# A third buffer of xs, moved bias sums, and v and the output product as three fp32r passes

## The reference

```python
x = x + 0.5 * ffn(layernorm(x))           # ffn: sum of 8 selected 256x256 adapters, gated, plus bias
x = x + attn(layernorm(x))                # an RWKV block, below
x = x + 0.5 * ffn(layernorm(x))

# attn(x):
h = layernorm(x, ln1_g, ln1_b); hh = time_shift(h)
xk, xv, xr = (h * m + hh * (1 - m) for m in (tm_k, tm_v, tm_r))
k, v, sr = xk @ Wk.T, xv @ Wv.T, sigmoid(xr @ Wr.T)
x = x + (sr * wkv(time_decay, time_first, k, v)) @ Wo.T     # wkv: a recurrence over the 512 tokens
h = layernorm(x, ln2_g, ln2_b); hh = time_shift(h)
xk, xr = (h * m + hh * (1 - m) for m in (cm_k, cm_r))
kv = square(relu(xk @ Wck.T)) @ Wcv.T                       # 256 -> 1024 -> 256
return x + sigmoid(xr @ Wcr.T) * kv
```

## Time and profile before

| | us |
|---|---|
| median of 3 runs (442.34, 442.79, 445.81) | 442.79 |
| profiled execution, whole time | 446.01 |
| its span, first to last instruction | 444.1 |
| PE busy | 428.9 (97%) |
| DVE busy | 379.5 (85%) |
| ACT busy | 298.8 (67%) |
| POOL busy | 179.6 (40%) |

### The profile page before, as it was taken

One profiled execution on the slowest core, in us unless ns is written; L12 is line 12 of the kernel. 1 busy time (PEld: TensorE's weight loads), 2 busy tenths in 40 slices (PEclk: granted clock), 3 DMA queues, 4 the chain that ended last, 5 costly groups with the idle time before them and its releaser, 6 DMA issues. The chain is left out here.

```text
span 444.1 us, 6141 instructions
## 1 busy us (share of the span) xinstructions
PE 428.9 (97%) x2014; PEld 335.3 (76%) x2014; DVE 379.5 (85%) x764; ACT 298.8 (67%) x558; POOL 179.6 (40%) x164
## 2 busy tenths in 40 slices
PE   8989999989999999999999899999999999999996
PEld 8865875578858885798759785788569875988985
DVE  3989988979989998999899998999899989976235
ACT  1158979874779568884889477965886487926510
POOL 1535063426271645445363627154543436133011
PEclk9999999969999999999999999999999999999998
DMA  6991010001000200011001100010001000000101
GB/s 199 384 397 41 1 47 0 0 2 50 0 0 1 95 1 1 0 49 48 1 0 47 50 1 1 0 47 2 0 2 47 1 1 0 26 22 1 47 2 48
DMA packets 15970, 18.51 MB, mean 42 GB/s; under 512 B 1082, under 2 KB 13634, under 8 KB 15938
## 3 DMA queue, kind: packets, MB, share of 16 engines
q1 hardware_dynamic: 14538, 17.05, 10.8%
q10 hardware_dynamic: 1400, 1.07, 0.9%
HBM read 13.92 MB, written 4.19 MB: 41 GB/s over the span
## 5 line engine op out<-in xcount | busy, mean ns | idle before, releaser
L448 PE MATMUL pair<-wcv_sb,kk 128*128 128x256 f32 x448 | 100.5, 380 | 0.0
L448 PEld LDWEIGHTS pair<-wcv_sb,kk 128*128 128x128 f32 x448 | 84.5, 191 | 10.9
L1224 POOL TENSOR_TENSOR x2b<-xs,bias_bc 128x512 f32<-128x512 f32 (+1 forms) x16 | 20.2, 1265 | 97.8 <-DVE xs L1047 48.6
L418 PE MATMUL pair<-xck_hi,wck_hi 128*128 128x512 f32 x128 | 57.9, 452 | 0.0
L422 PE MATMUL pair<-xck_lo,wck_hi 128*128 128x512 f32 x128 | 50.6, 395 | 0.0
L419 PE MATMUL pair<-xck_hi,wck_lo 128*128 128x512 f32 x128 | 50.6, 395 | 0.0
L617 ACT ACTIVATE h<-pair,vec 128x512 f32<-128x512 f32 x16 | 11.6, 774 | 45.7 <-PE pair L319 45.7
L673 ACT ACTIVATE kk<-pair 128x512 f32<-128x512 f32 x64 | 36.4, 593 | 8.6 <-PE pair L422 8.6
L677 ACT ACTIVATE kk<-kk 128x512 f32<-128x512 f32 x64 | 37.8, 639 | 0.5
L1264 POOL TENSOR_TENSOR xs<-x,xa 128x512 f32<-128x512 f32 x16 | 20.3, 1270 | 42.1 <-DVE xa L978 38.6
L1250 POOL TENSOR_TENSOR xr<-xr,h 128x512 f32<-128x512 f32 x16 | 18.6, 1181 | 41.5 <-ACT xr L718 41.5
(11 more groups left out here) (149 smaller groups left out, 1050.7 us busy)
## 6 DMA issues: line engine op xcount, KB each, us to landing
x<-in_x_dram SPq DMA_DIRECT2D x8, 512.0 KB, 3.5
out_dram<-xs SPq DMA_DIRECT2D x15, 256.0 KB, 2.1
xt<-in_xt_dram SPq DMA_DIRECT2D x4, 512.0 KB, 7.8
work<-in_ffn_w_dram ACTq DMA_DIRECT2D x4, 256.0 KB, 4.9
work<-in_ffn_w_dram SPq DMA_DIRECT2D x4, 256.0 KB, 5.0
kk<-in_wck_dram SPq DMA_DIRECT2D x1, 1024.0 KB, 10.1
xs<-in_xt_dram SPq DMA_DIRECT2D x2, 512.0 KB, 11.2
wcv_sb<-in_wcv_dram SPq DMA_DIRECT2D x1, 1024.0 KB, 13.0
```

Source lines behind the costliest of these rows:

```text
L418: nc.tensor.matmul(key_bank(n), wck_hi[:, h, cols], xck_hi[:, h, :], start=h == 0, stop=False)
L448: last = nc.tensor.matmul(bank_of("kv", e, i)[:, t % TB * C:(t % TB + 1) * C], kk[:, n, tok:tok + P], wcv_sb[:, n, :], start=n == 0, stop= ...
L1224: nc.gpsimd.tensor_tensor(dst, tile, bias_bc[:, :].rearrange("p (a c) -> p a c", a=1).broadcast_to([P, tiles, C]), ALU.add).then_inc(done, 1)
```

## The change

- `xs` has three buffers (`XS = 3`); the waits on the stores follow.
- v of sequences 1 to 7 becomes three fp32r passes. ACT makes `xv_hi` (`value_input_high`), DVE `xv_lo` (`value_input_rest`), both in two halves. The weights are split once (`setup_wv`, `value_weight_rest`).
- The output product of sequences 1 to 7 becomes three fp32r passes: `rwkv_hi` on ACT (`output_input_high`), `rwkv_lo` on DVE (`output_input_rest`). On PE it moves from behind four parts of value tile 0 to behind six.
- On DVE `gate_input_rest` (xcr_lo) moves from behind the exponent scans to ahead of x2t_lo; `add_second` is split around rwkv_lo.
- On ACT the squares of the keys move back, the relu of keys 6 and 7 ahead of the time gate, and the two gate tanh apart.
- On POOL the bias sum of x2 half 0 is released by xcr_lo, that of x half 0 by the last sum scan (`aa_done`), that of x half 1 by rwkv_lo.
- Several new tiles lie in the place of others (`in_place_of`), which adds waits.

```diff
+    XS = 3
@@ PE, front_v, for f > 0 @@
+                for o in range(CH):
+                    take(pair_of("v", f), o, t1_done, 2 * f + o + 1)
+                    cols = slice(o * P, (o + 1) * P)
+                    for h in range(CH):
+                        if o == 0:
+                            pe.wait_ge(xv_hi_done, 2 * (f - 1) + h + 1)
+                        nc.tensor.matmul(bank_of("v", f, o), wv_hi[:, h, cols], xv_hi[:, h, :], start=h == 0, stop=False)
+                        nc.tensor.matmul(bank_of("v", f, o), wv_lo[:, h, cols], xv_hi[:, h, :], start=False, stop=False)
+                        if o == 0:
+                            pe.wait_ge(xv_lo_done, 2 * (f - 1) + h + 1)
+                        last = nc.tensor.matmul(bank_of("v", f, o), wv_hi[:, h, cols], xv_lo[:, h, :], start=False, stop=h == CH - 1)
@@ PE, output_product, for f > 0 @@
+                pe.wait_ge(rwkv_lo_done, 2 * (f - 1) + 2)
+                for i in range(BANKS):
+                    take(pair_of("o", f), i, xa2_done, 2 * f + i + 1)
+                    for t in range(TB):
+                        last = three_passes(bank_of("o", f, i)[:, t * C:(t + 1) * C], i * TB + t, rwkv_hi, rwkv_lo, wo_hi, wo_lo)
@@ PE, the loop over e @@
-                channel_values(e, 0, range(HB // 2))
+                channel_values(e, 0, range(HB - 2))
                 if has(f):
                     output_product(f)
-                channel_values(e, 0, range(HB // 2, HB))
+                channel_values(e, 0, range(HB - 2, HB))
@@ ACT @@
+            def value_input_high(f):
+                for h in range(CH):
+                    act.wait_ge(xv_done, 2 * f + h + 1)
+                    if h == 0:
+                        act.wait_ge(gated_done, 2 * (f - 1) + 2)
+                    nc.scalar.activation(xv_hi[:, h, :], xv[:, h, :], ACT.Copy).then_inc(xv_hi_done, 1)
+            def output_input_high(f):
+                act.wait_ge(r_ps, 2 * f + 2)
+                for h in range(CH):
+                    act.wait_ge(rwkv_done, 2 * f + h + 1)
+                    nc.scalar.activation(rwkv_hi[:, h, :], rwkv[:, h, :], ACT.Copy).then_inc(rwkv_hi_done, 1)
@@ DVE @@
+            def value_input_rest(f):
+                for h in range(CH):
+                    dve.wait_ge(xv_hi_done, 2 * (f - 1) + h + 1)
+                    nc.vector.tensor_tensor(xv_lo[:, h, :], xv[:, h, :], xv_hi[:, h, :].bitcast(F32), ALU.subtract).then_inc(xv_lo_done, 1)
+            def output_input_rest(f):
+                for h in range(CH):
+                    dve.wait_ge(rwkv_hi_done, 2 * (f - 1) + h + 1)
+                    nc.vector.tensor_tensor(rwkv_lo[:, h, :], rwkv[:, h, :], rwkv_hi[:, h, :].bitcast(F32), ALU.subtract).then_inc(rwkv_lo_done, 1)
@@ POOL, the loop over e @@
                 if has(e - 1):
+                    pool.wait_ge(xcr_lo_done, 2 * e + 2)
+                    bias_to_x2(e - 1, 0)
+                if has(f):
                     mix_r(f)
                     hold_exponents(f)
-                if has(e - 1):
-                    if has(f):
-                        pool.wait_ge(aa_done, 2 * f + 2)
-                    bias_to_x2(e - 1, 0)
                 if has(f + 1):
-                    pool.wait_ge(rwkv_done, 2 * f + 2)
+                    pool.wait_ge(aa_done, 2 * f + 2)
                     bias_to_x(f + 1, 0)
+                    pool.wait_ge(rwkv_lo_done, 2 * (f - 1) + 2)
                     bias_to_x(f + 1, 1)
```

More of the change, by code:

```diff
@@ L76, in build @@
         x1 = [sb(f"x1_{i}", [P, NT, C]) for i in range(X1)]
-        xs = [sb(f"xs_{i}", [P, NT, C]) for i in range(2)]
+        xs = [sb(f"xs_{i}", [P, NT, C]) for i in range(XS)]
         xa = sb("xa", [P, NT, C])
@@ L121, in build @@
         xcr = sb("xcr", [P, CH, T])
+        xcr_lo = in_place_of("xcr", "xcr_lo", [P, CH, T])
         kk = sb("kk", [P, HB, T])
@@ L128, in build @@
         rwkv = sb("rwkv", [P, CH, T])
+        rwkv_hi, rwkv_lo = in_place_of("xr", "rwkv_hi", [P, CH, T]), in_place_of("rwkv", "rwkv_lo", [P, CH, T])
+        xv_hi, xv_lo = in_place_of("thr", "xv_hi", [P, CH, T]), in_place_of("xv", "xv_lo", [P, CH, T])
         work = sb("work", [P, 8 * CH * PAD])
@@ L152, in build @@
         xt_loaded = [sem(f"xt_loaded_{b}") for b in range(B)]
-        stored = [sem(f"stored_{i}") for i in range(2)]
+        stored = [sem(f"stored_{i}") for i in range(XS)]
         bn_done = {k: sem(f"bn_done_{k}") for k in kinds}
@@ L294, in _ @@
                 sp.wait_ge(x3_done, 2 * LAST + j + 1)
-                sp.dma_start(some_tiles(tok_dram(out, LAST), j), some_tiles(xs[LAST % 2], j)).then_inc(stored[LAST % 2], 16)
-            sp.wait_ge(stored[(LAST - 1) % 2], 16 * BANKS * (B // 2))
-            sp.wait_ge(stored[LAST % 2], 16 * (BANKS * (B // 2 - 1) + len(LAST_PARTS)))
+                sp.dma_start(some_tiles(tok_dram(out, LAST), j), some_tiles(xs[LAST % XS], j)).then_inc(stored[LAST % XS], 16)
+            for i in range(XS):
+                sp.wait_ge(stored[i], 16 * sum(len(LAST_PARTS) if b == LAST else BANKS for b in range(i, B, XS)))
         @block.tensor
@@ L330, in to_tokens, with three_passes @@
                     last.then_inc(filled, 1)
-            def three_passes(dst, t):
+            def three_passes(dst, t, own_hi, own_lo, w_hi, w_lo):
                 tok = slice(t * P, (t + 1) * P)
-                passes = [(x2t_hi[:, h, tok], w[:, h, :]) for h in range(CH) for w in (ffn_hi, ffn_lo)]
-                passes += [(x2t_lo[:, h, tok], ffn_hi[:, h, :]) for h in range(CH)]
+                passes = [(own_hi[:, h, tok], w[:, h, :]) for h in range(CH) for w in (w_hi, w_lo)]
+                passes += [(own_lo[:, h, tok], w_hi[:, h, :]) for h in range(CH)]
                 for j, (own, other) in enumerate(passes):
@@ L344, in second_tokens @@
                     for t in range(TB):
[L345 removed]
+                        last = three_passes(bank_of("y2", b, i)[:, t * C:(t + 1) * C], i * TB + t, x2t_hi, x2t_lo, ffn_hi, ffn_lo)
                     last.then_inc(y2_ps, 1)
@@ L431, in channel_gate @@
                     for t in range(TB):
[L432 to L435, removed]
-                            last = nc.tensor.matmul(bank_of("cr", e, i)[:, t * C:(t + 1) * C], own, other, start=j == 0, stop=j == len(passes) - 1)
+                        last = three_passes(bank_of("cr", e, i)[:, t * C:(t + 1) * C], i * TB + t, xcr_hi, xcr_lo, wcr_hi, wcr_lo)
                     last.then_inc(cr_ps, 1)
@@ L677, in key_square, with channel_gate @@
                 nc.scalar.activation(kk[:, n, :], kk[:, n, :], ACT.Square).then_inc(sq_done, 1)
-            def channel_gate(e):
+            def channel_gate(e, part):
                 if e > 0:
                     act.wait_ge(x2_done, 2 * (e - 1) + 2)
-                for i in range(BANKS):
+                for i in part:
                     act.wait_ge(cr_ps, 2 * e + i + 1)
@@ L797, in _ @@
                     rough_reciprocal(f)
-                    time_gate(f)
                 key_relu(e, 6)
                 key_relu(e, 7)
-                for n in range(HB // 2, HB):
+                if has(f):
+                    time_gate(f)
+                for n in range(1, HB // 2):
                     key_square(e, n)
-                channel_gate(e)
+                channel_gate(e, (0,))
+                for n in range(HB // 2, HB - 2):
+                    key_square(e, n)
+                if has(f):
+                    output_input_high(f)
+                channel_gate(e, (1,))
                 if has(f):
                     residual_of(f)
+                for n in range(HB - 2, HB):
+                    key_square(e, n)
                 if has(f + 2):
@@ L1155, in _ @@
                     add_second(e - 1, 0)
+                if has(f):
+                    output_input_rest(f)
+                if has(e - 1):
                     add_second(e - 1, 1)
```

120 lines of the change are left out of this document (79 added, 41 removed).

## The result

The changed kernel takes 453.2 us (median of 4 runs, 453.1 to 453.7), the kernel before 442.62 beside it: ratio 1.0211, 95% interval 1.0168 to 1.0255. The interval lies above 1 as a whole, so the change is slower; whether by more than 2% it leaves open. The profiled execution took 453.27, with a span of 451.5 where before it was 444.1.

The account below looks back on a forecast made before the run. DVE's way from value sum to norm was taken as the bound, PE's work barely covering it. 446.0 + 9.0 (stages 1 to 5) + 1.1 (stage 6) - 1.2 (stage 0) = 454.9, or 454.1 from the median; forecast 454, range 449 to 459.

Parts of the forecast that it names:

- PE's gain of 1.22 a stage: PE, output product and v as three passes: 0.62 and 0.60 us less work a stage.
- DVE's first part, +1.0: DVE, value sum to second state scan: xv_lo ahead of the exponent scans makes it 1.0 us later (0.9 to 1.2).
- DVE's second part: DVE, rwkv's end to output sum: 4.87 us against 4.06, +0.8 (0.4 to 1.3), including 0.1 waiting for rwkv_hi.
- PE's waits of 1.7: PE stops about 1.7 us each ahead of the output product (for rwkv_lo) and the turn of xa (for the norm).
- A growth of 1.8 in each of the stages 1 to 5: Middle stages: DVE's 1.0 plus 0.8 lengthen each by 1.8 us, 9.0 in sum.
- only one of the two DVE terms: Rival: the other DVE term falls into an unseen wait or the collision goes wholly; 445 to 449 us, say 447; chance 0.14.
- The clock: Rival: PE's new waits lower its clock, 2.4 us in each of six stages; 469 us; chance 0.06.
- Stage 0, -1.2: Stage 0: relus come earlier, PE's gate wait shrinks from 3.09 to about 1.8; -1.2 us (-2.4 to +1.8).
- Stage 6, +1.1: Stage 6, where PE sets the length: output product starts 1.7 us later and is 0.62 shorter, +1.1.
- The third xs buffer, nothing: Stores from xs: no wait on a store stands in the loop, so a third buffer changes nothing.
- The range: Whole kernel: 449 to 459 us for the forecast case, from the ends of the two DVE terms.
- The row on the collision: First ffn's sum on DVE beside POOL's second bias sum: one instruction took 1371 ns, others 470; 0.50 of 0.90 us regained.

Follow-up runs that it names:

- e5: The changed kernel with xcr_lo put back between the exponent scans and the state scans; 457.68 us, ratio 1.0297 to the kernel before.
- e6: The kernel before with only xcr_lo moved ahead of x2t_lo on DVE; 441.04 us, ratio 0.9945 to the kernel before.
- e4: The changed kernel with seven unused identity multiplications on PE ahead of its wait for the turn of xa; 448.77 us, ratio 1.0101 to the kernel before.
- e7: The changed kernel with six of eight parts of the third value tile ahead of the turn of xa; 451.19 us, ratio 1.0180 to the kernel before.
- e2_v_plain: The changed kernel with v back in plain f32, the output product still in three passes; 446.41 us, ratio 1.0050 to the kernel before.
- e11_both_plain_four_parts: The changed kernel with v and output product plain f32, the output product behind four value parts; 437.43 us, ratio 0.9857 to the kernel before.

## Why the prediction was right, and where not

The forecast was 454, the measurement 453.2. That they lie so close is luck: the sum doesn't hold term by term.

- *PE's gain of 1.22 a stage*: right. Stage 1 has 46.55 of work, has 47.74.
- *DVE's first part, +1.0*: wrong. The first exponent scan came 10.31 behind the value sum (forecast 10.4), but the second state scan 16.90, not 17.8. The step that failed is the sentence "That xcr_lo no longer stands behind the scans does not give this back". It gave nearly all of it back: the clamp of 2.90 had been lengthened by xcr_lo itself, a row I had only read in the other direction, as what the clamp does to the state scan. e5 and e6 show it both ways.
- *DVE's second part*: right, 4.84 for a forecast of 4.87, with no wait for rwkv_hi.
- *PE's waits of 1.7*: 1.57 ahead of the turn, but 0.68 ahead of the output product, where the missing 1.0 of the first part is lacking.
- *A growth of 1.8 in each of the stages 1 to 5*: 0.87 at whole clock. By this term alone it would have been the rival "only one of the two DVE terms", at 447.
- *The clock*, a rival at 0.06: it decided in three stages of five, at 1.7 and not 2.4 each. Growth and falls make 9.7 over these stages, against undisturbed ones of 48.07, near the 9.0 I had for another reason.
- *Stage 0, -1.2*: -0.82. PE waits 0.71 at the gate and the clock stays whole there, where before the wait was 3.09. Against an execution without that fall of 2.4 it is an estimated +1.6, near the +1.2 of the sum from the median. *Stage 6, +1.1*: -0.29; PE's wait for rwkv_lo there is 0.53 and not 1.7, and I had set only the output product's gain against it.
- *The third xs buffer, nothing*: the sentence that no wait on a store stands in the loop overlooks stage 3, where POOL stood 3.15 for one, which made that stage 0.87 longer in the one profiled execution. e6_xcr_forward, with two buffers too, shows no such wait.
- *The range*: the ends of the two DVE terms, 1.3 to 2.5 a stage, give 451.5 to 457.5 around 454; 449 to 459 is wider than the source it names.

So direction and mechanism (PE freed, DVE's way longer, PE waiting at both places) held, and the time came out by two errors that cancel: a growth set twice too large, and a clock set whole. e4 shows the size without the falls: 448.77, just outside the range.

The row on the collision has a rule beside it. The Trainium skill, SBUF — State Buffer, section "SBUF: two separate sides", says that whichever of a DVE instruction with two SBUF inputs and a GpSimd instruction starts first gets the shared ports for the whole instruction. e7 agrees, with 2.48 and 3.24; and a clamp of 2.90 beside xcr_lo, 2.01 without, is the direction of that rule which the prediction left out. The state scan, which reads two SBUF tiles, doesn't follow it: in the change it lies wholly inside the clamp (178.26 for 1.23 in 177.63 for 2.01), and takes no longer than the second one, behind the clamp (1.22). So the 0.4 of the earlier trace rows that the prediction put down to the clamp isn't the clamp's alone: the scan takes 1.63 only where xcr_lo stands just ahead of it, and what lengthens it there no run settles.

## What to carry to other kernels

When an operation moves, cost what it leaves as well as where it lands: look at which engine's row was long because it lay there. Work taken from an engine that is barely the longest turns into a wait on it, and a wait of TensorE can cost more than its own length through the clock. An edit that fills a wait shifts everything behind it, and two operations that had just missed each other may meet: a semaphore that puts them behind each other was worth 5.5 us here (439.99 to 434.51).

## What was not expected of the hardware

- A clamp on POOL (one tile read) took 2.01 with a DVE scan wholly inside it, and 2.90 when it started beside a DVE subtraction of two SBUF tiles, in the middle stages of every run that placed them so.
- The same stop of PE lowers the clock sometimes: with waits of 1.55 to 1.85 ahead of the turn, it fell in 3 of 5 stages of the change, in 1 of 5 of e2_v_plain, and in 5 of 5 of e5_xcr_back, which has a wait of 1.15 some 9 us before, in the profiled executions. Waits of 0.65 to 1.15 alone lowered it in no middle stage. Ahead of the stages, too, a wait of 1.04 left it whole, and one of 1.77 in e4_fill and e11_both_plain_four_parts was followed by a fall. The Trainium skill, TensorE: Matmul & The Clock Gate, section "Part 1: The HAM clock gate (the "warmup" mystery)", says that the chip's monitor runs free of the program, so that the same kernel can meet it differently. The executions of one kernel agree with that: those of e2_v_plain had a granted clock of 0.992 to 1.000, those of e5_xcr_back 0.980 to 0.992. What makes one of two equal waits fall isn't settled here.
